# Two transformer layers on one core: the preparation merged into the token program, the first expert's weights and tables moved ahead of the experts' program

## The reference, cut to what matters

```python
x = x + tanh(g_xattn[0]) * memory_xattn(ctx, layernorm(x), conv_w, conv_b)   # shifts and compresses the memory
x = x + tanh(g_ffn[0]) * (quantised(layernorm(x)) @ quantised(weight).T + bias)
x = x + tanh(g_xattn[1]) * cross_attention(layernorm(x), ctx, U_w, D_param)
x = x + tanh(g_ffn[1]) * experts(layernorm(x), Wr, W1, W2)                   # 8 experts, the top one is taken
```

## Time and profile before

| what | value |
|---|---|
| median of 3 runs | 2247.3 us (2244.41 to 2247.98) |
| the profiled execution's own time | 2244.2 us |
| its span | 2242.5 us |
| PE busy | 1988.4 us, 89% |
| VectorE, ScalarE, GpSimd busy | 1055.7, 797.9, 681.2 us |
| mean granted TensorE clock | 0.955 of full speed |

### The profile page before, as it was taken

The page is one execution under the profiler, slowest core; times in us unless marked ns, Lnnn a source line. Parts: engine busy times, 40 slices in busy tenths (PEclk is TensorE's granted clock), DMA queues, the critical chain, the costliest instruction groups (busy, mean ns, idle before and its releaser), DMA issues.

```text
span 2242.5 us, 35473 instructions
## 1 busy us (share of the span) xinstructions
PE 1988.4 (89%) x11356; PEld 1694.7 (76%) x11357; DVE 1055.7 (47%) x2310; ACT 797.9 (36%) x1548; POOL 681.2 (30%) x587
## 2 busy tenths in 40 slices
PE   2358889989988985399999999999999999999997
PEld 2146677767776764288898999899889899889987
DVE  4177898899889743614242113211422413312241
ACT  2134656665566543314132113211422312311241
POOL 0143344343434212515243113311522412311250
PEclk9669999999999985599999999999999999999999
DMA  6221333233333223714243013300421501411130
GB/s 169 100 68 38 112 120 137 104 127 118 131 112 124 74 77 132 231 39 141 79 131 101 19 37 102 117 28 28 140 90 42 173 24 63 139 33 37 45 116 18
DMA packets 152195, 208.42 MB, mean 93 GB/s; under 512 B 12782, under 2 KB 78574, under 8 KB 152149
## 3 DMA queue, kind: packets, MB, share of 16 engines
q1 hardware_dynamic: 111077, 114.14, 15.9%
q0 software_dynamic: 15728, 43.38, 6.2%
q10 hardware_dynamic: 25344, 50.33, 6.2%
HBM read 140.98 MB, written 68.37 MB: 93 GB/s over the span
## 4 chain that ended last, share of the span: by engine, by line
PE 56%; issue 1%; DMA 1%; POOL 1%; ACT 1%; DVE 0%; POOLq 0%; DVEq 0%; ACTq 0%
PE bank L1546 23%; PE bank L1554 22%; PE bank L1519 5%; PE bank L1499 5%; PE bank L1477 1%; PE bank L1508 1%; POOL w_lo L1291 0%; DMA tgu<-t_d,idx_tu 0%; PE bank L1483 0%; ACT w_hi L1411 0%; ACT w_hi L1412 0%; DMA out_dram<-obu,idx_xu 0%; POOLq L1209 0%; DVE xg L1704 0%; POOL out_dram L1281 0%
## 5 line engine op out<-in xcount | busy, mean ns | idle before, releaser
L1640 DVE SCALAR_TENSOR_TENSOR hT_lo<-bank,hT_hi 128x256 fp32r<-128x256 f32 x352 | 149.2, 424 | 656.9 <-ACT hT_hi L1442 634.3
L1442 ACT ACTIVATE hT_hi<-bank 128x256 fp32r<-128x256 f32 x352 | 135.2, 384 | 749.3 <-PE bank L1546 735.3
L1546 PE MATMUL bank<-inT_hi,w_lo 128*128 128x256 f32 x1408 | 398.5, 283 | 0.0
L1546 PE MATMUL bank<-inT_lo,w_hi 128*128 128x256 f32 x1408 | 398.3, 283 | 0.0
L1546 PE MATMUL bank<-inT_hi,w_hi 128*128 128x256 f32 x1408 | 396.8, 282 | 0.0
L1554 PE MATMUL bank<-w_hi,hT_hi 128*128 128x512 f32 x704 | 279.9, 398 | 0.0
L1546 PEld LDWEIGHTS bank<-inT_hi,w_hi 128*128 128x128 f32 x1408 | 269.0, 191 | 13.3
L1546 PEld LDWEIGHTS bank<-inT_lo,w_hi 128*128 128x128 f32 x1408 | 269.0, 191 | 12.0
L1554 PE MATMUL bank<-w_lo,hT_hi 128*128 128x512 f32 x704 | 277.7, 394 | 0.0
L1554 PE MATMUL bank<-w_hi,hT_lo 128*128 128x512 f32 x704 | 274.1, 389 | 0.0
L1546 PEld LDWEIGHTS bank<-inT_hi,w_lo 128*128 128x128 f32 x1408 | 269.0, 191 | 0.0
(11 more groups left out here) (263 smaller groups left out, 3916.1 us busy)
## 6 DMA issues: line engine op xcount, KB each, us to landing
stage<-in_L_ffn_W_dram SPq DMA_DIRECT2D x256, 256.0 KB, 2.9
X<-in_x_dram SPq DMA_DIRECT2D x16, 1024.0 KB, 5.1
t_d<-tt ACTq DMA_DIRECT2D x16, 1024.0 KB
x_d<-x ACTq DMA_DIRECT2D x16, 1024.0 KB
out_dram<-y ACTq DMA_DIRECT2D x16, 1024.0 KB, 4.3
xs<-in_x_dram SPq DMA_DIRECT2D x16, 768.0 KB
cw<-in_L_xattn_conv_w_dram SPq DMA_DIRECT2D x1, 4096.0 KB, 33.9
xs<-in_x_dram SPq DMA_DIRECT2D x16, 128.0 KB
```

The source lines that it names most:

```text
L1442: act.activation(hT_hi[:, f % 4, :], hb[f % 4][:, 0:CN], ACT.Relu).then_inc(e_hh, 1)
L1546: last = pe.matmul(hb[f % 4][:, 0:CN], l[:, k, fs], r[:, k, :], start=(n == 0), stop=(n == 3 * KB - 1))
L1640: dve.scalar_tensor_tensor(out=hT_lo[:, f % 4, :], in0=hb[f % 4][:, 0:CN], scalar=0.0, in1=hT_hi[:, f % 4, :].bitcast(F32), op0=ALU.max, o ...
```

## The change: what it does, and the diff

- The blocks of preparation and tokens become one: each engine's preparation steps now stand ahead of or between its first rounds, and in place of the barrier each engine waits for counts (`convolved`, `prepared`, `stored`) before a certain round. On ScalarE and VectorE stage z of group 0 is done amid the preparation.
- SP's loads have a new order: gates, `xc`, `conv_w` in four transfers, group 0's `xs` and `X`, then the rest, the transposed small ones (`dp`, `km`) late. `comp_d` is written before `cx_d` and `uq_d`, and group 1 is loaded between.
- The subtraction for `cx_hl` (L390) and the multiplication that restores `wf` (L410) go from VectorE to GpSimd (now L529, L533).
- `stage` gets an address that is free of other use once `xs`, `n1` and `xdT` are done with; SP loads the first 8 blocks of the first expert there at the end of the token program, after waits for `g_x1`, `p_bt` and `p_bm`.
- The tables are planned at the end of the token program's VectorE stream; `planned` goes.
- In the experts' program ScalarE splits six blocks before it turns to the unit's input, and VectorE makes the low parts of both W1 and W2 for the first expert (`split_first`), six blocks ahead of the input and ten behind it. GpSimd's `split_w1(0)` goes; for the other experts nothing changes.

```diff
+        def convolved(eng):
+            for s, value in ((k_pe, pe_at["comp"]), (w_comp, 16), (w_init, 48)):
+                eng.wait_ge(s, value)
+        def prepared(eng):
+            for s, value in ((k_dve, len(DVE_STEPS)), (k_act, len(ACT_STEPS)), (k_pe, len(PE_STEPS)),
+                             (k_cxlo, B), (w_comp, 16), (w_init, 48)):
+                eng.wait_ge(s, value)
+        def stored(eng):
+            for s, value in ((w_cx, 16), (w_uq, 16)):
+                eng.wait_ge(s, value)
...
 @block.sync
-            batch(0)
+            sp.dma_start(g_raw[:, 0:2], row(g_xattn).broadcast_to([P, 2])).then_inc(l_gate, 16)
...
+            sp.dma_start(xc[:, :, :], x[:, HALF:HALF + CW, :].rearrange("b s d -> s b d")).then_inc(l_xc, 16)
+            for r in range(RATE):
+                half_r = (cw_a, cw_b)[r // (RATE // 2)]
+                sp.dma_start(half_r[:, r % (RATE // 2), :, :], cwv[r, :, :, :]).then_inc(l_cw[r], 16)
+            load_group(0, 0)
...
+            sp.wait_ge(k_dve, dve_at["comp"])
+            sp.dma_start(comp_d[:, :], comp).then_inc(w_comp, 16)
+            sp.wait_ge(w_comp, 16)
+            load_group(0, 1)
...
             with sp.Fori(1, B) as b:
                 batch(b)
+            for f in range(RING):
+                if f == 0:
+                    sp.wait_ge(g_x1, NG)
+                if f == RING // 4:
+                    sp.wait_ge(p_bt, T * NG)
+                if f == RING // 2:
+                    sp.wait_ge(p_bm, T * NG)
+                load_weight_block(sp, 0, f)
 @block.gpsimd
-            pipeline(pool, body)
...
+            pool.wait_ge(l_cx, 16)
+            for b in range(B):
+                pool.wait_ge(k_act, act_at[f"cxhi{b}"])
+                pool.tensor_tensor(cx_hl[:, b, 1, :], cx[:, b, :], cx_hl[:, b, 0, :].bitcast(F32),
+                                   ALU.subtract).then_inc(k_cxlo, 1)
+            pool.wait_ge(k_dve, dve_at["wq8"])
+            for k in range(KB):
+                pool.tensor_tensor(wf[:, k, :].rearrange("p (n c) -> p n c", c=BLK),
...
+                                   ALU.mult).then_inc(k_wdq, 1)
+            convolved(pool)
+            pipeline(pool, body, 0)
 @block.vector
-            pipeline(dve, body)
...
+            body(*groups(0))
+            dve.wait_ge(l_small, 64)
+            step("gbias", dve.tensor_scalar(gbias[:, :], fb_raw[:, :], gates[:, 2:3], None, ALU.mult))
...
+            convolved(dve)
+            body(*groups(1))
+            prepared(dve)
+            body(*groups(2))
+            stored(dve)
+            pipeline(dve, body, 3)
             slots_of(NG - 1)
...
+            dve.memset(onesc, 1.0).then_inc(c_one, 1)
+            dve.wait_ge(c_tot, 1)
...
  @block.scalar
-                planned(act)
+                for f in range(6):
+                    split_high(0, f, None)
                 unit_inputs(0)
                 chunk_inputs(0)
-                for f in range(FB):
+                for f in range(6, FB):
                     split_high(0, f, None)
  @block.vector
+                def split_first(f):
+                    fs = slice(f * P, f * P + P)
+                    dve.wait_ge(e_hi, 2 * f + 1)
+                    dve.tensor_tensor(w1_lo[:, :, fs], w1_block(f), w1_hi[:, :, fs].bitcast(F32),
+                                      ALU.subtract).then_inc(e_split[f % RING], 1)
+                    split_w2(0, f)
...
+                for f in range(6):
+                    split_first(f)
                 unit_inputs(0)
                 chunk_inputs(0)
...
-                for f in range(FB):
-                    split_w2(0, f)
+                for f in range(6, FB):
+                    split_first(f)
```

More of the change, by code:

```diff
@@ L108, in flamingo_two_layers @@
         counts = sb("counts", [P, E], F32)
+        with nc.sbuf_tensor("stage", [P, RING, 2, D], F32) as stage:
+            pass
         tok = ExitStack()
@@ L536, in flamingo_two_layers @@
+        below = scratch(2 * (E + 1) * E)
+        first = scratch(2 * (E + 1))
+        coef = scratch(2 * (E - 1))
+        shift0 = scratch(1)
+        cidx = scratch(CI)
+        moved = scratch(2 * CI)
+        hit = scratch(2 * (E - 1) * CI)
+        c_one, c_tot, c_v, c_io = (sem("c_" + n) for n in ("one", "tot", "v", "io"))
         token_block = ExitStack()
@@ new lines, in _ @@
+            load_group(0, 0)
+            sp.dma_start(fb_raw[:, :], row(ffn_b).broadcast_to([P, D])).then_inc(l_small, 16)
+            sp.dma_start(cb_raw[:, :], row(conv_b).broadcast_to([P, D])).then_inc(l_small, 16)
+            sp.dma_start(wf[:, :, :], ffn_w.rearrange("(k p) i -> p k i", p=P)).then_inc(l_wf, 16)
+            sp.dma_start(uf[:, :, :], u_w.rearrange("(k p) i -> p k i", p=P)).then_inc(l_uf, 16)
+            sp.dma_start(cx[:, :, :], ctx.rearrange("b l d -> l b d")).then_inc(l_cx, 16)
@@ new lines, in _ @@
+            for h in range(KB):
+                pe.wait_ge(k_dve, dve_at["cxT3"] if h < 2 else dve_at[f"uqf{h - 2}"])
+                hs = slice(h * P, h * P + P)
+                for k in range(KB):
+                    for n, (a, c) in enumerate(((uw_hi, cxT_hi), (uw_hi, cxT_lo), (uw_lo, cxT_hi))):
+                        last = pe.matmul(bank[bank_of[f"uq{h}"]][:, 0:B * L], a[:, k, hs], c[:, k, :],
+                                         start=(k == 0 and n == 0), stop=(k == KB - 1 and n == 2))
+                last.then_inc(k_pe, 1)
@@ new lines, in _ @@
+            q8w = wq8[:, :, :].rearrange("p k (n c) -> p (k n) c", c=BLK)
+            step("wq8", dve.tensor_tensor(q8w, wblocks, bc(win), ALU.mult, saturate=False))
+            dve.wait_ge(k_pe, pe_at["comp"])
+            step("comp", dve.tensor_tensor(comp, bank[7][0:B * TC, :], cb_raw[0:B * TC, :], ALU.add))
+            low_parts("uw", uw_hi, uw_lo, D)
+            low_parts("cxT", cxT_hi, cxT_lo, B * L)
+            for h in range(KB):
+                dve.wait_ge(k_pe, pe_at[f"uq{h}"])
+                step(f"uqf{h}", dve.tensor_scalar(uqf[:, h, :], bank[bank_of[f"uq{h}"]][:, 0:B * L], 0.0,
+                                                  dp[:, h:h + 1], ALU.max, ALU.mult))
```

761 lines of the change are left out of this document (361 added, 400 removed).

## The result

The changed kernel takes 2197.78 us (median of 4 runs, 2196.92 to 2200.4) against 2247.64 for the kernel before in the same comparison: ratio 0.9782, 95% interval 0.9765 to 0.9799. The profiled execution has a span of 2194.6 us (before 2242.5), 47.9 less, where I had forecast 36.9.

A forecast was written before the change was run, and what follows sets the result against it. PE was taken to stand still at two places, the opening and 901 to 931 us. 2244.2 - 16.0 - 20.9 = 2207.3 us, 2210.4 from the median, stated as 2209; own range 2203 to 2216, wider 2196 to 2224.

The forecast's parts named there:

- L: Opening: moment the small transposed loads (`dp`, `km`) have landed and `gbias` can start; 51 us, bounds 35 and 58.
- a faster one: Rival: the opening's loads run at 300 GB/s, L 43.8, opening gives 23, second place 24; 2197 to 2200 us; chance 0.18.
- the opening: Kernel start up to `g_x1` of group 0, then group 1's `xs` load: `g_x1` at 80.2 instead of 96.24, gain 16.0 us.
- the second place: Start of the experts' program, PE nearly idle from 901 to 931 us: first chunk at 950 instead of 970.88, gain 20.9.
- The slower ring: Rival, opening: loads slower than assumed, L 62 to 67, opening gives 0 to 5 us; total 2221 to 2226; chance 0.13.
- dragging tiny loads: Rival, opening: `dp` and `km` drag the loads under 120 GB/s; at 100 GB/s 41 us lost, total 2267; chance 0.03.
- From L to `g_x1`: Opening: serial VectorE then GpSimd work after L, ending with `X` of group 0; 29.2 us, so `g_x1` at 80.2.
- The barrier: End of token program: 9.0 us of planning hidden under last writes and barrier, experts begin at 901.0 as before.
- The first expert: Barrier exit to first chunk: 49 us instead of 69.9, from an earlier gather, VectorE's low parts and no `tgu` wait.
- VectorE holds GpSimd back: Rival, first expert: 12 low parts delay the idx copy and first gather, 5 us later, total 2214; chance 0.17.
- Low parts of 0.68: First expert: each VectorE low part takes 0.68 us without GpSimd at work; 12 take 8.2, 20 take 13.6.
- the rival that they stay at 1.67: First expert: low parts slow from weights landing in `stage`, not GpSimd; first chunk at 976, total 2236; chance 0.05.

The follow-up runs named there:

- e2: The changed kernel without the eight weight blocks loaded in the last rounds, all sixteen of the first expert loaded after the barrier: 2203.6 us against 2197.8.
- e6: The changed kernel with the small transposed loads `dp` and `km` issued third and fourth instead of behind 10.2 MB: 2193.0 us against 2197.8.
- e7: The changed kernel with the 109-row piece of `xs` loaded as 64 and 45 rows, other groups' pieces cut in two as well: 2191.9 us against 2197.8.
- e9: The changed kernel with two GpSimd waits added every round: `gbias` addition after VectorE's `nb_a`, n products after all four `q`: 2182.6 us against 2197.8.
- e4: The changed kernel with only the merged preparation kept, the experts' start put back as before the change: 2220.4 us against 2197.8.
- e3: The changed kernel with the tables planned behind the barrier, at the head of the experts' program: 2206.6 us against 2197.8.
- e8: The changed kernel with the first expert's blocks 6 and 7 split between the unit's and chunk's inputs on ScalarE and VectorE: 2197.3 us against 2197.8.
- e1: The changed kernel with the first expert's W1 low parts back on GpSimd: 2206.6 us against 2197.8.
- e5: The changed kernel with GpSimd's addition of `xs` to group 0's `X` moved ahead of its `cx_hl` and `wf` work: 2193.8 us against 2197.8.
- e10: The changed kernel with the four edits of e5, e6, e7 and e8 together: 2185.2 us against 2197.8.
- e12: e10 plus only the first wait of e9, GpSimd's `gbias` addition waiting for `nb_a`: 2171.4 us, 15.4 under e10 by the spans.

## Why the prediction was right, and where its sum was not

**L, the moment of `gbias`: 51 forecast, 43.0 measured.** This is the term that was mis-sized, and most of the difference: 8.0 of 11.0 us by the spans. I carried 241 GB/s over from the kernel before; the ring gave 313 from 12 to 38 us, with the engines busy 0.98 of the time instead of 0.90. Both factors moved: 9% by fewer idle engines, and the rest because a busy engine moved 20 GB/s instead of 16.7 (313 / 16 / 0.98). 43 was inside my bounds (35 to 58), but "`gbias` before 44" was among my own signs of being wrong, and 2197.8 us lies outside the forecast's own range (2203 to 2216) and inside the wider one (2196 to 2224). What came was the rival "a faster one", chance 0.18, priced at L = 43.8 and 2197 to 2200. That its total fits so closely is in part luck: the opening gave 25.3 and not 23, the rounds 1.1 and not nothing, and the second place 21.5 and not 24. Why a busy engine moved more was not tried. `conv_w` is four transfers of 1 MB now and one of 4 MB before, in another order of its dimensions, which may be it; e2's 317 GB/s shows only that the rate is no exception.

**The slower ring and the dragging tiny loads.** Refuted: the ring gave 313 GB/s, and in e6, where `dp` and `km` stand at its head, they cost 1.9 us. The rule by which `xc` on four engines would make L about 56 did not show in L; e7 bears out the rule for the 109 rows, but what `xc` costs was not tried. One sum there is off: by the prediction's own formula L is 92 at 120 GB/s and passes 88 at 126. Nothing hangs on it.

**From L to `g_x1`: 29.2 forecast, 27.2 measured.** GpSimd's products for `wf` took 1.01 us each and not 1.31, and 1.31 is what such products take beside VectorE's `q`: the row I had used held the very contention that e9 removes. That is 1.2 of the 2.0; the steps up to GpSimd took 13.6 and not 14.2. The load of group 1's `xs` took 15.7 for 15.0. Together, 8.0 + 2.0 - 0.7, the opening gave 25.3 instead of 16.0, and e4 shows that this passes whole to the end.

**The barrier.** Planning under it costs nothing, as forecast (e3), and the exit moved with the rounds.

**The first expert: exit + 49 forecast, + 48.3 measured**, by errors that cancel, which is luck. The chunk's low input was ready at exit + 19 (893.7, from which the low parts run on) and not + 15.7. The two gathers landed 6.91 us after the last one's issue (882.74), where I had used the 4.9 of the first gather in the kernel before. The 20 low parts behind the input took 12.1 us and not 16.1: they run 0.60 apart, and GpSimd took nothing from them, since it was itself shut out. The 2.5 I had added for its instructions was on the wrong side.

With that the low parts are no longer what ends last. They end at 905.7, and PE comes to `hidden(3)` only at 907.88, without a wait on them. What held it before was `hu` (until 904.27), which stands in ScalarE's queue behind the ten blocks of high parts, 892.73 to 903.23. I had put those down as "earlier"; here they set the moment, 2.2 us behind the low parts. From `hidden(3)` to the first chunk it took 15.1 us and not 17.0, at a granted clock of 1.00 (907.9 to 923.0), where in the kernel before it was 0.54 just behind the wait for `tgu` (963.3 to 967.0). Who wants to shorten this place further must shorten ScalarE's part too; e8 took from both engines.

**VectorE holds GpSimd back: 0.17, forecast to cost 5.** It happened, but at another place. Ahead of the first gather VectorE ran 12 low parts, also 0.60 apart, and yet GpSimd got in (`idx_tu` 0.41 instead of 0.19, the gather 1.13 instead of 1.08; the 1.44 of the earlier trace rows was a gather as well, and not a write). The 8.60 us fell on `idx_xu`, behind which the second unit's rows are gathered, and they were still in time for their turn at 916.65.

**Low parts of 0.68**, against the rival that they stay at 1.67: right. The weights land in `stage` here too (218 GB/s from 876 to 923 us) and the parts take 0.68; with W1's low parts back on GpSimd (e1) single ones take up to 11.03. **The load ahead**, costed at nothing: wrong, it is worth 5.8 to 7.5 us (e2), which the estimate of exit + 49 held without saying so, since it let the low parts run at VectorE's own pace. **From the first chunk to the end**: 1271.6, right.

## What to carry to other kernels

Read a duration's smallest value beside its mean: a 128x4 product with a mean of 1.5 us and a minimum of 0.16 is a wait that no view lists as one, and here it and its like held 51 us of VectorE's time. When a serial preparation is put under a stream of loads, find the last small load that the chain needs and issue it early; here that cost the stream 1.9 us and not the 8 I had feared. And what an early wait gives back is found only by following the chain to the next engine: e5 got 5.3 us by the spans for a wait of 9.43, e9 less than a third of the busy time.

## What the runs showed of the hardware that I had not expected

A shut-out can last for a whole run of the other engine's instructions: 8.60 us for a copy behind 14 of VectorE's low parts, and in e8, e10 and e12, where it began later in the same run, 4.58, 6.11 and 4.90, each time to the run's end, within 0.1 us; 11.03 us for a low part behind GpSimd's products in e1. But it need not: at 877.55 a copy got in between low parts that were spaced just as closely, and in the kernel before the two engines took turns, 1.67 each. ScalarE, on which each low part also waits, was only just ahead of VectorE in those two places and further ahead in the others, which may decide it; no run was made to settle that. A piece of 109 rows also holds up SP: the issue of the next transfer took 3.68 us, and 0.25 when the piece was cut (e7).
